# Layer 1's attention: the sum of negated maximum and q made by GpSimd instead of VectorE

## The reference

```
q = x @ Wq.T
k = jnp.concatenate([x_text @ Wk.T, x @ Wk.T], axis=1)
v = jnp.concatenate([x_text @ Wv.T, x @ Wv.T], axis=1)
scores = jnp.einsum('bhnd,bhkd->bhnk', q, k) / jnp.sqrt(jnp.float32(d))
first = jnp.tanh(gate) * jnp.ones_like(scores[..., :1])
rest = jax.nn.softmax(scores[..., 1:], axis=-1)
attn = jnp.concatenate([first, rest], axis=-1)
out = jnp.einsum('bhnk,bhkd->bhnd', attn, v)
```

## Time and profile before

| | us |
|---|---|
| median of 3 runs (927.07 to 929.5) | 927.13 |
| the profiled execution | 930.15 |
| its span, first to last instruction | 928.4 |
| TensorE busy | 841.6 |
| VectorE busy | 763.0 |
| ScalarE busy | 555.4 |
| GpSimd busy | 309.8 |

### The profile page before, as it was taken

How to read it: one execution, slowest core, us unless ns; L and a number is a source line. 1 busy time by engine, 2 the same in 40 slices (tenths; PEclk the granted TensorE clock), 3 DMA queues, 4 the chain that set the end, 5 groups by cost and what they waited for, 6 DMA issues and landing times.

```text
span 928.4 us, 16914 instructions
## 1 busy us (share of the span) xinstructions
PE 841.6 (91%) x5288; PEld 651.5 (70%) x5288; DVE 763.0 (82%) x1907; ACT 555.4 (60%) x1077; POOL 309.8 (33%) x507
## 2 busy tenths in 40 slices
PE   5998887899999999999999999999979989978796
PEld 3776756666666665688878788778767779867574
DVE  6899899869999998699889899788887755465886
ACT  3777565547777775675666565577755534423474
POOL 2644226313444433232222122433421253321143
PEclk9999999759999997999999999999998999997998
DMA  5000000000000000010000000020001000000001
GB/s 155 9 2 1 4 26 1 25 1 26 26 25 26 22 23 1 9 42 0 1 1 1 1 1 1 0 76 2 1 2 43 1 1 1 1 1 1 1 12 34
DMA packets 26005, 14.12 MB, mean 15 GB/s; under 512 B 11047, under 2 KB 25406, under 8 KB 25918
## 3 DMA queue, kind: packets, MB, share of 16 engines
q1 hardware_dynamic: 25758, 13.04, 5.1%
q10 hardware_dynamic: 160, 0.00, 0.0%
HBM read 11.99 MB, written 1.05 MB: 14 GB/s over the span
## 4 chain that ended last, share of the span: by engine, by line
PE 47%; DVE 8%; issue 3%; ACT 3%; POOL 0%; DVEq 0%; ACTq 0%; POOLq 0%
PE bank L1844 4%; PE bank L1846 3%; PE bank L1845 3%; PE bank L798 2%; PE bank L1319 2%; PE bank L1900 2%; PE bank L1901 2%; PE bank L1899 2%; PE bank L1274 2%; PE bank L1284 2%; PE bank L1297 1%; PE bank L1255 1%; PE bank L731 1%; PE bank L709 1%; PE bank L758 1%
## 5 line engine op out<-in xcount | busy, mean ns | idle before, releaser
L893 ACT ACTIVATE L_pt<-bank 128x512 f32<-128x512 f32 x224 | 127.2, 598 | 46.4 <-PE bank L767 32.5
L515 POOL TENSOR_TENSOR L_kc<-L_kc_all,const 128x256 fp32r<-128x256 f32 x96 | 59.7, 625 | 141.7 <-PE bank L767 81.9
L1026 DVE TENSOR_REDUCE L_ms<-bank 128x2 f32<-128x512 f32 x128 | 84.0, 685 | 11.8 <-PE bank L716 11.4
L1801 POOL TENSOR_TENSOR L1f_xg_lo<-L1f_xg_raw,L1f_xg_hi 128x512 fp32r<-128x512 f32 x32 | 42.0, 1313 | 145.3 <-ACT L1f_xg_hi L1949 141.3
L880 ACT ACTIVATE L_part<-bank,L_bias_ca,const 128x256 fp32r<-128x256 f32 x128 | 68.9, 563 | 33.8 <-PE bank L687 32.4
L2065 DVE TENSOR_TENSOR L1f_h_lo<-L1f_h,L1f_h_hi 128x512 fp32r<-128x512 f32 x88 | 75.2, 859 | 6.2 <-ACT L1f_h_hi L1954 5.9
L1943 ACT ACTIVATE L1f_a<-bank 128x512 f32<-128x512 f32 x88 | 52.4, 599 | 43.3 <-PE bank L1846 42.9
L1024 DVE TENSOR_REDUCE L_mc<-bank 128x8 f32<-128x512 f32 (+1 forms) x96 | 65.1, 678 | 8.7 <-PE bank L709 4.4
L1954 ACT CAST L1f_h_hi<-L1f_h 128x512 fp32r<-128x512 f32 x88 | 54.3, 618 | 18.8 <-DVE L1f_h L2060 18.8
L716 PE MATMUL bank<-L_k,L_q 32*128 32x256 f32 x256 | 55.9, 342 | 5.1 <-DVE L_ms L1026 4.9
L887 ACT ACTIVATE L_hm<-bank,const 128x256 fp32r<-128x256 f32 x96 | 45.6, 475 | 21.5 <-PE bank L731 20.6
(11 more groups left out here) (427 smaller groups left out, 2601.1 us busy)
## 6 DMA issues: line engine op xcount, KB each, us to landing
L_raw<-in_L_ffn_w_dram SPq DMA_DIRECT2D x8, 176.0 KB, 2.3
L_raw<-in_L_ffn_v_dram SPq DMA_DIRECT2D x8, 176.0 KB, 2.5
L_raw<-in_L_ffn_w_dram SPq DMA_DIRECT2D x6, 192.0 KB, 2.9
x<-in_x_dram SPq DMA_DIRECT2D x4, 256.0 KB, 4.3
mask<-in_mask_Bx1xSxS_ff_dram SPq DMA_DIRECT2D x2, 512.0 KB, 5.6
out_dram<-x SPq DMA_DIRECT2D x4, 256.0 KB, 2.3
const<-in_const_dram SPq DMA_DIRECT2D x1, 964.0 KB, 6.0
ctx_rows<-in_ctx_dram SPq DMA_DIRECT2D x1, 256.0 KB, 3.1
```

Source lines behind the costliest of these rows:

```text
L515: pool.tensor_tensor(kc[:, g], kc_all[:, g, bass.ds(b, 1)].bitcast(F32).to_broadcast([P, GH, S2]), pr.c("head4").unsqueeze(2).to_broadcast ...
L893: act.activation(pt[:, g // 2, (g % 2) * NS + (HEADS_1[i] if own_keys else i)], b_st[(g * NS + i) % 2][:], ACT.Exp, scale=scale).then_inc( ...
L1026: dve.tensor_reduce(ms[:, :, i - 1], bank.rearrange("p (t s) -> p t s", s=S), AX_X, ALU.max).then_inc(sem["sc_taken"], 1)
```

## The change

VectorE's `maxima` loses its first addition and waits for the semaphore `hq_ready`; GpSimd gets a step `maxima` that makes this addition, behind ScalarE's copy. Since GpSimd works in order, the diff also says where in its queue the new steps stand. Outside layer 1 the new step is empty, and the edits of layers 0 and 2 leave GpSimd's order of instructions as it was.

```
@@ vector(dve), maxima(b, g)
             dve.wait_ge(sem["m_hi"], past["m_hi"] + b * NG + g + 1)
             need(dve, sem["st_done"], b * U + (g - 1) * NS, past["st_done"])
             if gated:
-                need(dve, sem["m_split"], b * NG + g, past["m_split"])
-                dve.wait_ge(sem["qk_split"], past["qk_split"] + b * NG + (g + 1))
-                dve.tensor_tensor(hq[:], hm[:], q[:, g].bitcast(F32), ALU.add).then_inc(sem["hq_ready"], 1)
                 dve.wait_ge(sem["hq_ready"], past["hq_ready"] + b * NG + (g + 1))
             dve.tensor_tensor(mt[:, g % 2], b_mt[:, 0:S], hq[:] if gated else hm[:], ALU.add).then_inc(sem["m_split"], 1)
@@ PLACES, "gpsimd"
-        (('att1', 'keys', 0, 3), *of("att1", ('p_bo',)), *of("ffn0", ('mul', 0), ('mul', 1), ('split', 0), ('mul', 2)), *of("att1", ('spread', 0), ('turn', 0), ('keys', 1, 0))),
-        (('att1', 'o_norm', 6), *of("ffn1", ('prepare',)), *of("att1", ('o_norm', 7))),
+        (('att1', 'maxima', 0, 1), *of("att1", ('p_bo',)), *of("ffn0", ('mul', 0), ('mul', 1), ('split', 0), ('mul', 2)), *of("att1", ('spread', 0), ('turn', 0), ('keys', 1, 0))),
+        (('att1', 'maxima', 7, 3), *of("ffn1", ('prepare',)), *of("att1", ('o_norm', 7))),
```

More of the change, by code:

```diff
@@ L516, in keys, with maxima @@
                                pr.c("head4").unsqueeze(2).to_broadcast([P, GH, S2]), ALU.mult).then_inc(sem["kc_ready"], 1)
+        def maxima(b, g):
+            if gated:
+                pool.wait_ge(sem["m_hi"], past["m_hi"] + b * NG + g + 1)
+                need(pool, sem["m_split"], b * NG + g, past["m_split"])
+                pool.wait_ge(sem["qk_split"], past["qk_split"] + b * NG + (g + 1))
+                pool.tensor_tensor(hq[:], hm[:], q[:, g].bitcast(F32), ALU.add).then_inc(sem["hq_ready"], 1)
         def values(b):
@@ L588, in o_norm @@
                 pool.tensor_tensor(rstdb[:], veb[:], pr.neg_half[:, 0:2], ALU.pow).then_inc(sem["o_rstd"], 1)
-        return {"p_rstd": p_rstd, "p_zero": p_zero, "p_bo": p_bo, "spread": spread, "turn": turn, "keys": keys, "mask": mask, "mask_in": mask_in, "o_norm": o_norm}
+        return {"p_rstd": p_rstd, "p_zero": p_zero, "p_bo": p_bo, "spread": spread, "turn": turn, "keys": keys, "mask": mask, "mask_in": mask_in, "o_norm": o_norm, "maxima": maxima}
     def tensor(pe):
@@ L3079 @@
         (('att0', 'keys', 0, 2), *of("att0", ('p_rstd', 1), ('turn', 0))),
-        (('att0', 'keys', 0, 3), *of("att0", ('keys', 1, 0))),
-        (('att0', 'turn', 1), *of("att0", ('keys', 1, 1))),
+        (('att0', 'maxima', 0, 0), *of("att0", ('keys', 1, 0))),
+        (('att0', 'maxima', 1, 0), *of("att0", ('keys', 1, 1), ('maxima', 1, 2))),
         (('att0', 'o_norm', 0), *of("att0", ('spread', 0))),
-        (('att0', 'keys', 6, 0), *of("ffn0", ('zero',))),
-        (('att0', 'keys', 7, 0), *of("ffn0", ('rstd', 0))),
+        (('att0', 'keys', 6, 0), *of("ffn0", ('zero',)), *of("att0", ('maxima', 7, 3))),
+        (('att0', 'maxima', 7, 1), *of("ffn0", ('rstd', 0))),
         (('att0', 'keys', 7, 3), *of("att0", ('spread', 7), ('o_norm', 7))),
@@ L3095 @@
         (('att2', 'keys', 1, 1), *of("att2", ('mask', 1))),
-        (('att2', 'keys', 1, 3), *of("att2", ('spread', 1), ('mask_in', 2), ('mask_in', 3))),
-        (('att2', 'mask', 2), *of("att2", ('turn', 1))),
-        (('att2', 'keys', 3, 0), *of("att2", ('turn', 2), ('o_norm', 0))),
+        (('att2', 'maxima', 1, 1), *of("att2", ('spread', 1), ('mask_in', 2), ('mask_in', 3))),
+        (('att2', 'mask', 2), *of("att2", ('turn', 1), ('maxima', 0, 2))),
+        (('att2', 'keys', 3, 0), *of("att2", ('turn', 2), ('maxima', 1, 2), ('o_norm', 0))),
         (('att2', 'o_norm', 1), *of("att2", ('spread', 2), ('mask_in', 4), ('keys', 3, 1))),
@@ L3101 @@
         (('att2', 'mask', 4), *of("att2", ('keys', 4, 2))),
-        (('att2', 'spread', 4), *of("att2", ('turn', 4), ('o_norm', 2))),
+        (('att2', 'spread', 4), *of("att2", ('turn', 4), ('maxima', 3, 2), ('o_norm', 2))),
         (('att3', 'keys', 0, 1), *of("att3", ('p_zero',), ('p_rstd', 1))),
```

## The result

The changed kernel takes 937.73 us (median of 4, 932.85 to 941.05), the kernel before, timed beside it, 927.37 (median of 4, 927.07 to 929.5): ratio 1.0103, interval 1.0055 to 1.015. Two more series of the unaltered changed kernel gave 1.0089 (1.0054 to 1.0125) and 1.008 (1.0046 to 1.0113). The forecast was 4.1 us; by the medians this series has 10.4, the two others 7.1 and 6.2. The direction and the places were right, the size was too small. The range went to 937: by the ratio the kernel takes 1.0103 times 927.13, 936.7, just inside, while the median of this series, 937.73, lies just outside.

What follows compares the result with a forecast made beforehand. VectorE, 28.6 of 30 us busy in the steady part, was taken to wait for hm rather than a free slot. Start 2.1, sequence 1 0.54, sequences 2 to 6 1.4, sequence 7 0.1: 4.1 on 927.13 gives 931.2, range 926 to 937.

Steps and rivals of the forecast that it cites:

- The addition and the way to GpSimd: From hm's end: 0.08 us from ScalarE to GpSimd, then 0.73 for GpSimd's addition, with ends 0.62 and 0.85.
- The way back to VectorE: Handoff from the end of GpSimd's addition to the start of VectorE's mt, taken as 0.04 us.
- point of decision: s is the time from hm's end to VectorE's addition; mt comes earlier only where s is over 0.40 us.
- A sequence in the steady part: Sequences 2 to 6: maxima 0 covered, maxima 1 0.04 us late, maxima 2 nothing, maxima 3 0.24; 0.28 per sequence.
- Sequences 1 and 7: Sequence 1: maxima 1 0.30 us late and maxima 3 0.24, together 0.54; sequence 7, mostly paced by TensorE: 0.1.
- The start: GpSimd's queued work delays mt 0,2 from 182.08 to 185.39 us, and TensorE's next projection by 2.1, counted in full.
- The steps moved past: GpSimd's keys b+1,0 and turn b+1 wait behind a maxima for some 3 and 1 us, at no cost.
- Slack (1): Existing waits and the stall near 185 us take up half of the sum, giving 929.2 us; chance 0.22.
- the freed slot (2): VectorE's freed 0.45 us pays: 912.7 us in full, 924.7 for a sixth of it; chance 0.05.
- the clock spared: An earlier mt 0,0 spares the low-clock stretch from 170 to 200 us, worth 8: 923 us; chance 0.06.
- The clock prolonged: The new stall at 185 us prolongs the lower clock level, costing 8 more: 939 us; chance 0.06.
- The fourth rival, hindrance: GpSimd and VectorE hinder each other, stretching 24 additions at full clock by 0.2 us each: 936 us; chance 0.07.

Runs made afterwards that it cites:

- no_sum: The changed kernel with the addition of q dropped on every engine, mt made of the bank and hm alone: ratio 0.993 to the kernel before.
- sum_on_tensor: The kernel before, with TensorE adding q into the bank by an identity product and the transposition made an accumulating product: ratio 0.999.
- change_third: The changed kernel unaltered, run a third time for its mean clock: ratio 1.008 to the kernel before.
- split_later: The changed kernel with GpSimd's split of expert 0 behind the sum of maxima 0,2 instead of ahead: ratio 1.0066 to the kernel before.
- Each half alone: The changed kernel with GpSimd making only sequence 0's sums (ratio 1.0002), or only those of sequences 1 to 7 (1.0023), VectorE the others.
- only_start: The changed kernel with GpSimd making only sequence 0's sums, VectorE all later ones: ratio 1.0002 to the kernel before.
- parts_first: The kernel before, with VectorE splitting the maximum into rounded part and rest before the transposition, without hm and hq: ratio 1.0156.
- longer_sum: The changed kernel with another 128x128 GpSimd addition ahead of each sum, 0.54 us more per step: ratio 1.0372 to the kernel before.
- change_again: The changed kernel unaltered, run again for its scatter: 937.94 us, ratio 1.0089 to the kernel before.

## Why the prediction was right, and where its size was off

- **What bounds the kernel: right.** VectorE was busy at 95%, and still its freed 0.45 was no gain, since hm comes from its own joined maximum. VectorE's 19.7 us of waiting for GpSimd, which itself stood and waited for hm 26 times of 32, are the plain sign, and no_sum prices the slot at 2.9 us for all 32. The chain from joined maximum to mt isn't the only bound either: in sum_on_tensor it is shorter and VectorE has less work, and the period grew.
- **The addition and the way to GpSimd: right.** 0.73 forecast, 0.729 measured; 0.08 forecast, 0.09 measured. The factor to VectorE is 1.75 (0.729 to 0.416), not the 2 that the Trainium skill gives (GPSIMD Engine Reference, section 8). That the total by the page's 2 would have been 5.5, as near to the measured 5.1 as the forecast's 4.1 or nearer, is luck: what was missing lay in the handoff, not in the addition.
- **The way back to VectorE: the mis-sized term.** The prediction took 0.04 from a small 128x4 instruction whose result VectorE reads the earlier trace rows; behind the 128x256 addition it is 0.13. That moves the point of decision from s = 0.40 to s = 0.49. It could have been seen: the same line L474 has another handoff in the kernel before, of 0.11 (656.98 to 657.09), and one row had been taken for the rule.

```profile
655.96 1.02 POOL L474 TENSOR_TENSOR L_rstd<-L_ve,neg_half 128x4 f32<-128x4 f32 x1
...
657.09 0.60 DVE L993 TENSOR_SCALAR L_xn<-x,L_mv,L_rstd 128x128 f32<-128x128 f32 x2 [1.65 <-POOL L_rstd L474]
```

- **A sequence in the steady part.** 0.28 was forecast, 0.49 measured. In change_third the lateness of mt against before grows by 0.06 at maxima 3,0, 0.17 at 3,1, 0.03 at 3,2 and 0.23 at 3,3. So maxima 1 costs 0.17 where 0.04 was forecast, and 0.09 of that is the handoff; maxima 0 is not quite covered; maxima 2 costs nearly nothing; maxima 3 costs 0.23 (0.24 forecast). For five sequences that is 2.5 instead of 1.4.
- **Sequences 1 and 7.** 0.64 was forecast. Sequences 1 to 7 cost 3.7 at equal clock, less 2.5 leaves 1.2. They were not measured apart. The trace of before has places that the prediction passed over: s was 0.03 at maxima 1,0 and 7,2, and 0.19 at 6,1 and 7,1 (sequence 6 is not quite like sequence 2).
- **The start: right.** 2.1 forecast, 1.9 ± 0.5 measured; split_later gives 2.2 of it back. The stall of over 3 us is there, with 4.46.
- **The steps moved past: right.** In neither trace does any engine wait for keys or for turn's addition to x.
- **The sum.** By the runs 5.1 at equal clock instead of 4.1. The rest of the measured difference, which was 6 to 10 us in the three series, goes with the clock, which the forecast left out of its main case: over all executions of both kernels 0.9524 less 0.9488 is 6.7 us more at the lower level, 2.5 us of time.
- **The rivals.** Slack (1) and the freed slot (2) fell. Of the third, the clock spared at the start was seen in one profile (the low stretch ended at 193 instead of 207 us, and another from 210 to 220 followed it). The clock prolonged, which had 0.06, is the direction that the means show, but in another place than the stall at 185 us: in the two other profiles the stretch there ends at 206 as before, and the additional one is at 287 to 305. Its price was also too low: the stretch of 34 us at the start of the layer costs 12.6 by the slope, and the 27.6 us of it in the 30 of the table 10.2, not 8.
- **The fourth rival, hindrance: nearly absent.** GpSimd's additions keep within 0.721 to 0.735. VectorE was held up beside one of them once, in the first profile: the normalisation of x at 204.66 took 0.68 instead of 0.34. The prediction's sentence that one addition ran beside a busy GpSimd and took 0.882 is not right as it stands: five more of the 32 overlapped with a GpSimd instruction, three of them by little more than 0.1 us or less, and took 0.411 to 0.425. The other hold-ups are beside GpSimd's split of the weights and come and go with the timing: the joined maximum, which has two SBUF inputs too, has a longest case of 0.771 before, 0.241 in the first changed profile, 0.46 in the two others. That instructions with two SBUF inputs collide with GpSimd's agrees with the Trainium skill (GPSIMD Engine Reference, section 8); that taking one such instruction away gained anything is not shown.
- **Open.** Whether the change lowers the mean clock, and by which part. Each half alone has a mean clock no lower than before (0.9538, 0.9534), the whole has 0.9488 and split_later 0.9463. That waits of TensorE spread over the sequences bring the low level on is argued, not shown, and the low stretches of only_start show that it would not be the only cause; scatter is not ruled out.

## What to carry to other kernels

Before an element-wise step is moved off the busiest engine, measure how long its input has been ready when the step starts. If that slack plus the time from the step's start to its reader's (here 0.45) is less than the other engine's way (here 0.09 + 0.73 + 0.13), the result comes later, however busy the engine that it leaves, and that costs time wherever no wait behind it covers it. An in-order queue that the step joins is priced by the longest block of work ahead of it at the one moment when the result is waited for, and an even comparison needs the mean granted clock beside each time.

## What the runs showed of the hardware

- The handoff from GpSimd to VectorE was 0.10 to 0.13 us behind the 128x256 addition, and 0.04 in one case and 0.11 in another behind the same 128x4 instruction; ScalarE to GpSimd was 0.08 to 0.09.
- VectorE's instructions with two SBUF inputs can be held up beside GpSimd's: 128x8 from 0.175 to 0.92 us (parts_first), 128x16 from 0.176 to 0.928 (longer_sum), 128x256 from 0.416 to 0.882 (before), the first two beside a two-input subtraction. Beside GpSimd's casts, which have one input, the 128x16 one took up to 0.46 (change_again). In the two cases shown it ended together with GpSimd's instruction, and the longest of a tiny instruction was as long as that of a large one. GpSimd's additions did not become longer.
- One us at the lower clock costs the kernel 0.37 us, over mean clocks from 0.919 to 0.961; if TensorE had set the pace all the time, half the clock would have made it 0.5. sum_on_tensor had the highest mean clock, 0.9611 against 0.9524 before; no run shows why.
